# Windowed attention and a top-2 mixture of experts on one core: a third round with V placed beside the second, tiles turned a step later, and V projected once a token and spread by DMA

## The reference

```python
Q = (x @ Wq.T).reshape(B, S, HKV=4, G=4, 8); K, V = (x @ Wk.T), (x @ Wv.T)  # reshape(B, S, 4, 8)
scores = einsum('bskgd,bswkd->bskgw', Q, K_win) / sqrt(8)   # window of 128 on either side, invalid = -inf
out    = einsum('bskgw,bswkd->bskgd', softmax(scores), V_win).reshape(B, S, 128) @ Wo.T
x = layernorm(x + out)
p = softmax(x @ router)                                     # 8 experts
w, i = top_k(p, 2); w = softmax(w)
y = sum over the two experts of w * (silu(x @ gate) * (x @ up)) @ down      # F = 256
x = layernorm(x + y)
```

## Time and profile before

| | |
|---|---|
| device time, median of 3 runs | 549.03 us (544.09, 549.03, 549.33) |
| device time of the profiled execution | 550.67 us |
| span of the profiled execution | 548.8 us |
| busy: PE, DVE, ACT, POOL | 483.2, 363.0, 294.6, 241.8 us |
| PE's share of the chain that ended last | 72% |
| bytes moved by DMA | 46.92 MB in 84156 packets |

### The profile page before, as it was taken

The page is one execution under the profiler, slowest core; times in us unless marked ns, Lnnn a source line. Parts: engine busy times, 40 slices in busy tenths (PEclk is TensorE's granted clock), DMA queues, the critical chain, the costliest instruction groups (busy, mean ns, idle before and its releaser), DMA issues.

```text
span 548.8 us, 11862 instructions
## 1 busy us (share of the span) xinstructions
PE 483.2 (88%) x3865; PEld 292.4 (53%) x3865; DVE 363.0 (66%) x823; ACT 294.6 (54%) x512; POOL 241.8 (44%) x329
## 2 busy tenths in 40 slices
PE   5699999999998999999999999987999999999700
PEld 2354454454453545344544554434788888888600
DVE  1556867867865446667767888755347765767785
ACT  2125655656655433446556666664565555655551
POOL 2501155455334030223284487600870727776772
PEclk9558999999999555779999999989999999999955
DMA  6633333342235215212621513102242555553462
GB/s 169 99 51 67 80 59 98 79 71 86 42 54 140 39 40 88 68 30 51 127 38 24 98 36 93 41 28 62 76 130 81 164 156 144 146 136 96 107 167 59
DMA packets 84156, 46.92 MB, mean 85 GB/s; under 512 B 40608, under 2 KB 79520, under 8 KB 83424
## 3 DMA queue, kind: packets, MB, share of 16 engines
q1 hardware_dynamic: 65360, 31.04, 25.7%
q0 software_dynamic: 4096, 8.40, 5.7%
q10 hardware_dynamic: 14640, 6.73, 4.4%
HBM read 26.47 MB, written 19.40 MB: 84 GB/s over the span
## 4 chain that ended last, share of the span: by engine, by line
PE 72%; DVE 8%; ACT 6%; POOL 5%; issue 5%; DMA 3%; ACTq 0%; SPq 0%; POOLq 0%; DVEq 0%
PE pV L811 15%; PE pX L736 6%; PE pX L775 6%; PE pX L1016 6%; ACT probs L1095 4%; PE pV L824 4%; PE pX L996 3%; PE pX L998 3%; PE pX L997 3%; PE pX L748 3%; PE pM L862 3%; PE pV L1007 3%; PE pX L787 2%; PE pM L830 2%; PE pX L766 2%
## 5 line engine op out<-in xcount | busy, mean ns | idle before, releaser
L1095 ACT ACTIVATE probs<-pX 128x1024 f32<-128x1024 f32 x152 | 152.9, 1024 | 73.4 <-PE pX L766 58.4
L1368 DVE TENSOR_REDUCE mp<-pX 128x4 f32<-128x1024 f32 (+4 forms) x128 | 150.7, 1185 | 41.0 <-PE pX L740 31.2
L811 PE MATMUL pV<-probs,vx 128*32 128x512 f32 (+1 forms) x736 | 96.1, 589 | 2.4 <-DVE attT L1419 2.0
L676 POOL DMA_INDIRECT probs<-ys,source x64 | 64.5, 1008 | 30.6 <-issue 25.7
L664 POOL DMA_INDIRECT xs<-xr,slot x64 | 63.0, 985 | 31.4 <-issue 17.6
L736 PE MATMUL pX<-kx,q 48*128 48x512 f32 (+4 forms) x256 | 63.3, 494 | 4.2 <-DMA q<-q_scr 4.0
L775 PE MATMUL pX<-q,kx 50*128 50x512 f32 x248 | 64.9, 520 | 0.5 <-DVE mp L1368 0.4
L1471 DVE TENSOR_TENSOR probs<-probs,pX 128x512 f32<-128x512 f32 x44 | 30.2, 686 | 34.4 <-ACT probs L1157 34.4
L1016 PE MATMUL pX<-we,probs 128*128 x352 | 47.0, 276 | 1.1 <-ACT vx L1169 1.1
L1016 PEld LDWEIGHTS pX<-we,probs 128*128 128x128 f32 x352 | 42.7, 192 | 2.0 <-issue 1.9
L1416 DVE RECIPROCAL rden<-pV 128x128 f32<-128x128 f32 x32 | 30.4, 951 | 18.8 <-PE pV L824 18.8
(11 more groups left out here) (151 smaller groups left out, 829.1 us busy)
## 6 DMA issues: line engine op xcount, KB each, us to landing
xt<-xs SPq DMA_DIRECT2D x88, 64.0 KB, 1.9
ys<-vx ACTq DMA_DIRECT2D x44, 128.0 KB, 2.1
q<-q_scr SPq DMA_DIRECT2D x42, 128.0 KB
xt<-xT SPq DMA_DIRECT2D x8, 512.0 KB, 5.7
q_scr<-qh SPq DMA_DIRECT2D x32, 64.0 KB, 2.3
q<-stage SPq DMA_DIRECT2D x128, 2.0 KB
xr<-x SPq DMA_DIRECT2D x8, 256.0 KB, 6.0
raw<-wgu SPq DMA_DIRECT2D x4, 512.0 KB, 5.9
```

Of the source, the lines that this page charges most:

```text
L676: pool.indirect_dma_start(yin[:, t % YIN, k, :], None, ys[ph][:, :], bass.IndirectOffsetOnAxis(ap=source[:, t, k:k + 1], axis=0), bounds_c ...
L811: mm = pe.matmul(pV[row:row + 32, cols], vx[:, chunk, pr, :], src[:, pr, cols], start=n == 0, stop=True, skip_group_check=True)
L1095: act.activation(dst, src[:], ACT.Exp).then_inc(exp_done, 1)
L1368: dve.tensor_reduce(mp[:, t % 2, 0, :, i, :], src[:, :, 0:2 * n].rearrange("p r (c v k) -> p r v c k", v=NV, k=32), AX.XY, ALU.max).then_i ...
```

## The change

1. PE: round 2 with V (and any further round) follows round 1 at once, ahead of maxima and turn; it stood behind A1. ACT's copy `po` moves ahead of `stage` and `x1T`.
2. `x_tile(s)` is s-7 in place of s-6: each turn is a step later. The logits keep their step.
3. xT is stored once. V is projected once a token: four products of 32 columns, copied by ACT (for n = 1 by DVE) into `vd` [128, 2, 4, 32]. SP writes it to `v_scr` in DRAM (`values_out`, in V's step) and reads it back by four DMAs of 32 partitions (`values_in`, a step later) into `vs`, and POOL spreads `vs` as before, two steps after V's step.
4. The pipeline's first step is -5, and V of group 1 is projected in step -3, ahead of all scores.

```diff
-FIRST = -4
+FIRST = -5
 def x_tile(s):
-    t = s - 6
+    t = s - 7
 # projected
-        for what, at in (("q", first), ("k", first + (1 if n == 1 else 2)), ("v", first + 3)):
+        for what, at in (("q", first), ("k", first + (1 if n == 1 else 2)), ("v", first + (2 if n == 1 else 3))):
+        vd = sb("vd", [P, 2, 4, 32])
 # sync: every load of xT is [128, GT] in place of [128, 2 * GT]
+            def values_out(n):
+                wait(sp, v_in[n % 2], 64 * (n // 2))
+                sp.dma_start(v_scr[n % 2].rearrange("(c p) e -> p c e", p=P), vd[:, n % 2]).then_inc(v_out[n % 2], 16)
+            def values_in(n):
+                sp.wait_ge(v_out[n % 2], 16 * (n // 2 + 1))
+                wait(sp, v_done, n)
+                for a in range(2):
+                    for o in range(2):
+                        row = 64 * a + 32 * o
+                        sp.dma_start(vs[row:row + 32, :, :], v_scr[n % 2].rearrange("(c a k) e -> a k c e", a=2, k=32)[a]
+                                     ).then_inc(v_in[n % 2], 16)
 # sync, step
+                for n in range(NGR):
+                    if s == (n - 2 if n < 2 else STEP_OF["v", n] + 1):
+                        values_in(n)
+                    if n and s == STEP_OF["v", n]:
+                        sp.wait_ge(m_evac, SMALL["v", n])
+                        values_out(n)
 # gpsimd
             def spread_values(n):
+                pool.wait_ge(v_in[n % 2], 64 * (n // 2 + 1))
...
-                if what == "v":
-                    pool.wait_ge(m_evac, SMALL["v", n])
-                    spread_values(n)
 # gpsimd, step
+                for n in range(NGR):
+                    if s == (n - 2 if n < 2 else STEP_OF["v", n] + 2):
+                        spread_values(n)
 # tensor
             def values_of(bank, n):
-                for c in range(8):
+                for c in range(4):
 # tensor, step
                 if has(s - 1):
-                    values(s - 1, 1)
+                    for n in range(1, len(rounds(s - 1))):
+                        values(s - 1, n)
...
                 a_item(s + 2, 1)
-                if has(s - 1):
-                    for n in range(2, len(rounds(s - 1))):
-                        values(s - 1, n)
                 b_item(s, 1)
 # scalar, project and step
-                    act.wait_ge(v_done, n)
-                    act.activation(vs[:].rearrange("p c e -> p (c e)"), pM[:, 0:256], ACT.Copy).then_inc(m_evac, 1)
+                    wait(act, v_out[n % 2], 16 * (n // 2))
+                    act.activation(vd[:, n % 2].rearrange("p c e -> p (c e)"), pM[:, 0:P], ACT.Copy).then_inc(m_evac, 1)
                 exps(s, 0)
+                if 0 <= s - 1 < NT:
+                    act.wait_ge(pv_done, ROUND_AT[s - 1, len(rounds(s - 1)) - 1])
+                    wait(act, nd_psum, s - 1)
+                    act.copy(po[:], pV[:]).then_inc(oT_done, 1)
...
-                if 0 <= s - 1 < NT:
-                    act.wait_ge(pv_done, ROUND_AT[s - 1, len(rounds(s - 1)) - 1])
-                    wait(act, nd_psum, s - 1)
-                    act.copy(po[:], pV[:]).then_inc(oT_done, 1)
 # vector, ahead of the steps
+            dve.wait_ge(m_psum, SMALL["v", 1])
+            dve.tensor_copy(vd[:, 1].rearrange("p c e -> p (c e)"), pM[:, 0:P]).then_inc(m_evac, 1)
```

More of the change, by code:

```diff
@@ L256, in k_ready, with attention_moe @@
     return 5 * n + 4
-def attention_moe(nc, x, xT, wq, wk, wv, wo, wr, wgu, wd, consts, out, q_scr, xs, ys):
+def attention_moe(nc, x, xT, wq, wk, wv, wo, wr, wgu, wd, consts, out, q_scr, v_scr, xs, ys):
     with ExitStack() as ctx:
@@ L358, in attention_moe @@
         v_done = sem("v_done")
+        v_out = [sem(f"v_out{i}") for i in range(2)]
+        v_in = [sem(f"v_in{i}") for i in range(2)]
         q_out = sem("q_out")
@@ L463, in _ @@
         def _(sp):
-            xg = xT.rearrange("d (n t) -> d n t", t=2 * GT)
-            sp.dma_start(xt[:, 0, :], xg[:, 0, :]).then_inc(xt_in, 16)
+            xg = xT.rearrange("d (n t) -> d n t", t=GT)
+            sp.dma_start(xt[:, 0, 0:GT], xg[:, 0, :]).then_inc(xt_in, 16)
             sp.dma_start(wq_sb[:], wq).then_inc(s_wq, 16)
@@ L470, in _ @@
             sp.wait_ge(xt_in, 16)
-            sp.dma_start(xt[:, 1, :], xg[:, 1, :]).then_inc(xt_in, 16)
+            sp.dma_start(xt[:, 1, 0:GT], xg[:, 1, :]).then_inc(xt_in, 16)
             def queries_out(n):
@@ L521, in step @@
                         sp.wait_ge(xt_in, 16 * (n + 1))
-                        sp.dma_start(xt[:, (n + 1) % 2, :], xg[:, n + 1, :]).then_inc(xt_in, 16)
+                        sp.dma_start(xt[:, (n + 1) % 2, 0:GT], xg[:, n + 1, :]).then_inc(xt_in, 16)
+                for n in range(NGR):
[4 more added lines that the diff above has]
+                        values_out(n)
                 if s % 4 == 0 and 0 <= s < NT:
@@ L543, in _ @@
             read_first_queries(sp, 2, 1, 4, q_in)
+            sp.wait_ge(v0_copied, 1)
+            values_out(0)
             for s in range(FIRST, NT):
@@ L625, in _ @@
             spread_keys(0, 1).then_inc(k_ops, 1)
-            pool.wait_ge(v0_copied, 1)
             pool.wait_ge(s_zero, 2)
-            spread_values(0)
             def norm(m):
@@ L857, in tokens @@
             def tokens(n):
-                return xt[:, n % 2, :].rearrange("p (c o k) -> p c o k", o=2, k=32)[:, :, 0, :]
+                return xt[:, n % 2, 0:GT]
             def values_of(bank, n):
-                for c in range(8):
+                for c in range(4):
                     mm = pe.matmul(bank[:, c * 32:(c + 1) * 32], xt[:, n % 2, c * P:(c + 1) * P], wv_sb[:],
@@ L1051, in _ @@
             act.wait_ge(p0_psum, 3)
-            act.activation(vs[:].rearrange("p c e -> p (c e)"), pX[1][:, 0, 0:256], ACT.Copy).then_inc(v0_copied, 1)
+            act.activation(vd[:, 0].rearrange("p c e -> p (c e)"), pX[1][:, 0, 0:P], ACT.Copy).then_inc(v0_copied, 1)
             act.wait_ge(k_ops, 2)
@@ L1590 @@
         "x": x,
-        "xT": np.ascontiguousarray(np.broadcast_to(
-            x.T.reshape(D, TOK // 32, 1, 32), (D, TOK // 32, 2, 32)).reshape(D, 2 * TOK)),
+        "xT": np.ascontiguousarray(x.T),
         "wq": np.ascontiguousarray(
@@ L1608 @@
     q_scr = nc.dram_tensor("q_scr", (2, 2, NR, 16, GT // 32, G, 32), F32, kind="Internal").ap()
+    v_scr = nc.dram_tensor("v_scr", (2, GT, KV * HD), F32, kind="Internal").ap()
     xs = [nc.dram_tensor(f"xs{b}", (ROWS, D), F32, kind="Internal").ap() for b in range(NPH)]
     ys = [nc.dram_tensor(f"ys{b}", (BLOCKS[b] * P, D), F32, kind="Internal").ap() for b in range(NPH)]
-    attention_moe(nc, *ins, out, q_scr, xs, ys)
+    attention_moe(nc, *ins, out, q_scr, v_scr, xs, ys)
     r = run_bass_kernel_spmd(nc, [arrays], core_ids=[0])
```

## The result

The changed kernel takes **521.72 us** (median of four runs, 516.93 to 526.01) beside 546.56 us (541.52 to 549.33) for the kernel before, run in turn with it. The ratio is 0.9526, 95% interval 0.9401 to 0.9651: faster, by about 25 us. The forecast was 524. The profiled execution is the fastest of the four: 516.93 us, span 515.1. So the two profiles lie 33.7 us apart, 9 us more than the medians, and what follows splits up the 33.7.

The account below looks back on a forecast made before the run. PE was taken to bound the kernel, by its work, its waits and its time at the low clock. Terms -17.5 - 3.0 - 5.4 - 3.4 + 2.1 + 0.6 = -26.6 from 550.67 us gave 524 us, range 517 to 531.

Parts of the forecast that it names:

- Clock, -17.5: PE from step 14 through 16: without the 1.90 us wait for POOL's tile the clock stays up, saving 17.5 us.
- The lower end, nothing: Low bound of the clock saving: zero, since the rows show only an order in time, not a cause.
- rival 1: The low-clock stretch comes all the same at the batch's edge, or as long elsewhere: 541 us, range 536 to 545, chance 0.24.
- Waits for turns, -3.0: PE's four waits for POOL's normalised tiles go, 3.0 us together.
- V projection, -5.4: Eight matmuls fewer on PE's path in each of six V steps, 0.9 us each: 5.4 us saved.
- Group 1 and the start, -3.4: Group 1's V moves ahead of the scores, 2.7 us saved; a smaller first load saves PE 0.7: 3.4 us.
- V rounds side by side, +2.1: Moving the third round ahead of A1 makes round 0 wait 0.3 us for DVE in seven plain steps: 2.1 us added.
- the same products: The third V round's products on PE take 0.57 us ahead of A1 just as between A1 and B1.
- DMA round trip, 0: V's extra write and four reads per group in SP's queue have a step of slack and cost nothing.
- Among the experts, +0.6: Tile 31's turn falls into step 38 with the logits that need it: 0.6 us added once, at most 1.5.
- rival 4: More clock than taken: earlier first rise, or no low stretch at 232 us; 517 us, to 514, chance 0.05.

Follow-up runs that it names:

- before_again: Unchanged copy of the kernel before, for a second profile: 689.37 us on a chip where the median of the kernel before is 678.76.
- after_again: Unchanged copy of the kernel after, for a second profile: 659.37 us beside 678.76 for the kernel before, ratio 0.9835.
- turn_only: Kernel before with only the turns of the normalised tiles a step later (s-7 for s-6): 537.06 us beside 546.54.
- rounds_only: Kernel before with only the V rounds side by side and the copy of `po` moved ahead on ACT: 533.22 us beside 546.54, ratio 0.9835.
- turn_back: Kernel after with only the turns back one step earlier (s-6): 527.02 us, ratio to the kernel before 0.9746.
- po_back: Kernel after with only the copy of `po` back behind the maxima's copy on ACT, rounds still side by side: 651.60 us beside 678.76, ratio 0.9698.
- rounds_back: Kernel after with the third V round back between A1 and B1 and the `po` copy back behind the maxima's: 525.81 us, ratio 0.9650.
- v_double: Kernel after with V's four pairs of matmuls of a group issued twice, the second four writing unread columns: 530.15 us, ratio 0.9827.
- xt_early: Kernel after with the load of the next group's tokens a step earlier, ahead of the queries' reads on SP's queue: 516.75 us beside 542.46, ratio 0.9648.

## Why the prediction was right, and where it was not

**Clock, -17.5: the size met in part by luck, the cause half right.** Turn, clock and V in steps 14 to 17 were to give 17.5 + 1.9 + 0.9 = 20.3 us. 25.4 came in the first pair of profiles, 13.9 in the second (before_again 60.80, after_again 46.91). turn_only shows that the late turn by itself takes away the wait and the long stretch in steps 14 and 15, for 13.4 us, and two profiles of each kernel agree on these two steps. But it is not the only edit that does: with the early turn, the joined rounds bring the stretch down to 10.2 us (rounds_only), and with the rest of the change besides none is left (turn_back). So it is still not shown that the wait brings the fall. The profiles show this much: a wait of 1.90 us had 47.8 us at half clock behind it twice, one of 1.47 us had 10.2 us once and nothing once, and without a wait for POOL there were 3.4 us once and nothing in nine profiles. The other 9.5 us, in steps 16 and 17, the late turn does not explain: turn_only took 29.42 us there, and the kernel after takes 21.07 in one profile and 29.57 in the next. That part of the profiled gain did not come from the edit; whether it was the execution's or the chip's is open, since po_back, on the chip of after_again, has the same falls. The lower end, nothing, and rival 1 named the right doubt: rows showed only an order in time. The clock stayed at 1.00 from 41 to 215 us as the forecast asked, but for the 3.4 us at 163.9. Of the ten profiles of kernels with the late turn none has a fall that begins in step 10 or 22, where turn and logits meet when the turn is early, while of the four with the early one before_again, rounds_only and turn_back do. The falls seen lie behind a short wait, or behind products of few columns (V, logits, ranks), or both, but so do many stretches without a fall; which of them decides, and why a stretch lasts 47.8 us here and 3.4 there, stays open. Stretches at half clock through which PE was all but fully busy, of 17.10 us in turn_only and 47.20 us in the kernel before, are in the traces.
The Trainium skill ("TensorE: Matmul & The Clock Gate", HAM oscillation — how this bites in real kernels) ties the falls to long stretches in which PE stands idle for a DMA; turn_only's fall at 195.2 us, out of a PE without a gap, is not of that kind. That sustained activity releases the low clock (the same page of the Trainium skill, What's actually happening) is what the two stretches just named speak against, if it is taken alone. In both the measurement decides.

**Waits for turns, -3.0: right.** All four are gone. turn_only is shorter by 0.67 us in step 6 and by 0.53 in each of steps 10 and 22, beside the 1.90 of step 14: 3.6 us.

**V projection, -5.4: right.** 10.92 to 10.04 us (before, rounds_back) and 9.78 to 10.67 (after, v_double): 0.88 and 0.89 us a V step where 0.9 was put.

**Group 1 and the start, -3.4: right.** From the maxima of tile 0 to those of tile 1 it is 8.51 to 5.75 us, -2.76 (put at 2.7); PE's first matmul comes 0.64 us earlier (0.7). Step 1 gave 0.54 back. -3.10 in all.

**V rounds side by side, +2.1: the wrong sign.** The step that failed is "the same products": 0.57 us between A1 and B1 was taken to cost 0.57 wherever it stands. It costs 0.67 there and 0.43 behind the other round. The new wait for DVE came in the plain steps and had the size that was put, 0.3 us, but it stands elsewhere: not round 0 waits for `attT`, whose waits are 2.0 us before and 2.1 after, but a B item waits until DVE has read the maxima out of its pair of banks. Step 6 of the kernel after:

```profile
93.34 0.50 PE L800 MATMUL pX<-q,kx 50*128 50x512 f32 x2 [0.34 <-DVE mp L1391]
```

Round 0 follows at 94.53, 3.65 us behind A1's end at 90.88 and without an idle ahead of it. The B item before the one shown starts some 0.2 us late too. Plain steps grow by only 0.05 us (8.95 in turn_only to 9.00), since the 0.24 saved, and 0.23 us that the step no longer waits for ACT, offset most of it. The K, V, Q and logits steps at full clock, where no such wait comes, got 0.25 to 0.34 us shorter: -5.5 us in 21 steps.

**DMA round trip, 0: missed.** V itself was never waited for. What it did to SP's queue was looked at only for the maxima; the load of the tokens, last behind the queries, was not. With steps 0.3 to 1.1 us shorter each, its slack was gone: 4.5 us of waits and a fall of the clock, some 6 us. In the kernel before the load stood in the same place, was issued at 120.84 us and landed 1.5 us ahead of its projection: the slower steps hid it. rounds_back and v_double, whose steps are longer, show no such wait, and xt_early takes it away.

**Among the experts, +0.6.** A wait of 0.45 us for ACT, as put; behind step 29 the kernel is 2.65 us shorter, of which a fall of 3.4 us at 361.7 us in before is the largest part that a row shows.

**The total.** 521.72 us lies 2.3 us below the forecast, and that is luck in part. Errors cancel: rounds -5.5 where +2.1 stood, tokens +6 where 0 stood. The clock term was met by one stretch that the edit takes away and one that came and went by itself. On the chip of after_again the same change is worth 1.65%, not 4.7%. Two small slips of the prediction changed nothing: the 7.8 us of rival 4 lead from 524 to 516.2, not 517, and the long fall begins at 177.4 us, not 177.7.

## What to carry to other kernels

The rounds with V cost 0.24 us less side by side than apart: count a block where it stands, with its neighbours. When an edit shortens every step, list each transfer with its slack against the shorter step, the ones that the edit doesn't touch above all. A fall of the clock behind a wait is a suspicion; a second profile of the same kernel tells what is its trait (14 and 15) and what is not (16 and 17). A wait that an edit is expected to make may show at another instruction of the same engine: look for it by what it waits for.

## What was not expected of the hardware

A matmul of 64 columns took nearly the time of one of 8 or of 32 (eight of them 1.10, 1.06 and 1.08 us from a 128x128 f32 stationary tile). The same load of tokens landed in 5.8 to 7.0 us behind six reads on its queue and in 2.9 to 3.4 us ahead of them. Between 50 and 260 us the time at half clock differed by a factor of ten between two profiles of one program (3 and 34 us), the second of them on a chip where everything takes longer.
